# An SSM layer and a top-4 mixture of experts on one core: work moved between the last sequences and the first expert tiles

## What is computed

```python
x = layernorm(x + mamba(x))          # 16 states per feature, scan over 512 tokens
x = layernorm(x + ffn(x))

# ffn: N = 4096 tokens, E = 8 experts, INNER = 512, TOP_K = 4
logits = x @ router_weight.T + router_bias
topk_logits, topk_idx = top_k(logits, 4); topk_w = softmax(topk_logits)
gate, up = split(x @ gate_up_proj[e].T + bias)
act = (clip(up, -7, 7) + 1) * min(gate, 7) * sigmoid(1.702 * min(gate, 7))
y[token] += topk_w * (act @ down_proj[e].T + bias)   # for each chosen expert e
```

## Time and profile before

| | |
|---|---|
| three runs | 1311.96, 1314.8, 1316.92 us; median 1314.8 |
| profiled execution | 1315.4 us, its span 1313.5 us |
| busy | PE 1167.2 us (89%), DVE 1052.3 (80%), ACT 884.6 (67%), POOL 740.5 (56%) |
| mean granted TensorE clock | 0.951 of full |

### The profile page before, as it was taken

One profiled execution on the slowest core, in us unless ns is written; L12 is line 12 of the kernel. 1 busy time (PEld: TensorE's weight loads), 2 busy tenths in 40 slices (PEclk: granted clock), 3 DMA queues, 4 the chain that ended last, 5 costly groups with the idle time before them and its releaser, 6 DMA issues. The chain is left out here.

```text
span 1313.5 us, 17907 instructions
## 1 busy us (share of the span) xinstructions
PE 1167.2 (89%) x5150; PEld 805.5 (61%) x5150; DVE 1052.3 (80%) x1816; ACT 884.6 (67%) x1518; POOL 740.5 (56%) x557
## 2 busy tenths in 40 slices
PE   9879897979799897697799999999999999999960
PEld 4324353535353443256688888888888888888850
DVE  4999999999999999988477766777667776677754
ACT  4685959494949585534466776777667777667744
POOL 0456567888787888875743344443444433444353
PEclk9899998999999898897989999999999999999995
DMA  3543435445454545547665655655556555565538
GB/s 124 191 162 134 172 128 204 171 162 180 176 193 172 192 140 191 208 144 278 198 167 163 164 131 141 166 163 164 133 138 167 164 162 140 135 162 165 162 40 264
DMA packets 69260, 217.21 MB, mean 165 GB/s; under 512 B 7520, under 2 KB 43232, under 8 KB 56288
## 3 DMA queue, kind: packets, MB, share of 16 engines
q1 hardware_dynamic: 33888, 171.61, 35.8%
q0 software_dynamic: 26880, 36.72, 16.2%
q10 hardware_dynamic: 8448, 8.39, 2.0%
HBM read 165.54 MB, written 51.15 MB: 165 GB/s over the span
## 5 line engine op out<-in xcount | busy, mean ns | idle before, releaser
L662 PE MATMUL p_y<-read,small 128*128 128x512 f32 x512 | 258.1, 643 | 57.3 <-POOL read L1290 57.1
L1098 DVE TENSOR_TENSOR_SCAN state<-decay,p_bu 128x512 f32<-128x512 f32 x256 | 297.1, 1201 | 2.9 <-ACT decay L858 1.7
L1619 POOL DMA_INDIRECT total<-o_v,tok x144 | 266.8, 1853 | 43.4 <-issue 43.3
L662 PEld LDWEIGHTS p_y<-read,small 128*128 128x128 f32 x512 | 101.7, 206 | 198.5 <-issue 115.0
L1617 POOL TENSOR_TENSOR scrap<-neg_half 128x1 f32<-128x1 f32 x36 | 14.1, 392 | 313.0 <-ACT o_v L1530 310.3
L858 ACT ACTIVATE decay<-dt,scan_rate 128x511 f32<-128x511 f32 x256 | 164.1, 710 | 13.9 <-DVE state L1098 13.6
L512 ACT ACTIVATE gate_v<-p_g,bias 128x512 f32<-128x512 f32 x144 | 98.3, 683 | 99.9 <-PE p_up L502 99.5
L533 ACT ACTIVATE ah<-a_v 128x512 fp32r<-128x512 f32 x144 | 91.1, 633 | 103.4 <-DVE a_v L526 103.4
L1337 POOL DMA_INDIRECT queues<-rows,index x128 | 134.7, 1052 | 36.8 <-issue 33.6
L1290 POOL TENSOR_TENSOR read<-state,bc 128x1024 f32<-128x1024 f32 x64 | 127.5, 2001 | 23.4 <-DVE p_bu L1089 11.6
L549 DVE TENSOR_TENSOR al<-a_v,ah 128x512 fp32r<-128x512 f32 x144 | 98.5, 685 | 12.4 <-ACT ah L533 12.4
(11 more groups left out here) (234 smaller groups left out, 2992.7 us busy)
## 6 DMA issues: line engine op xcount, KB each, us to landing
bc<-bc_rows SPq DMA_DIRECT2D x32, 1024.0 KB, 4.8
first_raw<-in_w_experts SPq DMA_DIRECT2D x19, 1668.0 KB, 6.8
raw_w<-in_w_experts SPq DMA_DIRECT2D x18, 1668.0 KB, 6.8
first_wh<-bc_rows SPq DMA_DIRECT2D x16, 1024.0 KB, 4.7
first_wl<-bc_rows SPq DMA_DIRECT2D x16, 1024.0 KB, 4.7
first_rows<-queues SPq DMA_DIRECT2D x19, 544.0 KB, 6.9
xq<-queues SPq DMA_DIRECT2D x18, 544.0 KB, 6.9
queues<-pad SPq DMA_DIRECT2D x9, 544.0 KB, 5.9
```

The lines of the kernel that those rows point to most:

```text
L662: mm = pe.matmul(p_y[h][:, :], ident[:, :], read[:, t % 4, h, :], start=False, stop=(t == SLOTS - 1))
L1098: dve.tensor_tensor_scan(state[t % 4][:, h, :], decay[t % AHEAD][:, h, :], p_bu[:, h * LEN:(h + 1) * LEN], 0.0, ALU.mult, ALU.add).then_in ...
L1619: pool.indirect_dma_start(total, bass.IndirectOffsetOnAxis(ap=tok[t.p][:, a:a + 1], axis=0), o_v[t.p][:, a, :], None, compute_op=ALU.add). ...
```

## The change

- The transposed rows of tile 1 are split into halves in round LAST, slot 3: ACT's two copies ahead of the copy of product 2 of tile 0, DVE's two subtractions ahead of its clips of chunks 2 and 3. Before, both stood in chunk 1 of tile 0's part of stage 2.
- `copy_tokens` moves on DVE from chunk 0 to chunk 2 of each tile, tile 0 among them.
- POOL issues eight of the last sequence's sixteen scatters in stage 1, and the other eight (`scatter_rest`) behind the adds of tile 0.
- The spare rows of `total` have a semaphore of their own, `s_spare`; POOL's stage 2 waits for it alone and no longer for the ends.
- `write_ends` moves on SP from behind the loads of tile 2 to behind the loads of tile 3.

```diff
@@ -385,7 +385,7 @@
     LAG = 2
     s_rows = [sem(f"s_rows{i}") for i in range(2)]
     s_tr, s_tok, s_share = sem("s_tr"), sem("s_tok"), sem("s_share")
-    s_ends = sem("s_ends")
+    s_ends, s_spare = sem("s_ends"), sem("s_spare")
     s_tload, s_plan, s_tables, s_pad = sem("s_tload"), sem("s_plan"), sem("s_tables"), sem("s_pad")
     s_w = [sem(f"s_w{i}") for i in range(2)]
     s_wh, s_wl, s_bias = sem("s_wh"), sem("s_wl"), sem("s_bias")
@@ -574,7 +574,7 @@
     def write_spare_rows(sp):
 
         sp.dma_start(queues[E * QUEUE:, :].rearrange("(p a) c -> p a c", a=SUBS), pad[:, :, :]).then_inc(s_pad, 16)
-        sp.dma_start(total[TOKENS:, :].rearrange("(p a) d -> p a d", a=SUBS), pad[:, :, 0:D]).then_inc(s_pad, 16)
+        sp.dma_start(total[TOKENS:, :].rearrange("(p a) d -> p a d", a=SUBS), pad[:, :, 0:D]).then_inc(s_spare, 16)
 
     def write_ends(sp, some):
 
@@ -924,6 +924,8 @@
                     for i in (2, 3):
                         read_gate(act, first, i)
                         read_up(act, first, i)
+                    for k in range(KD):
+                        copy_tile(act, second, k)
                     copy_product(act, first, 2)
                 if r.d and t == 3:
                     router_exp(r)
@@ -1246,6 +1248,8 @@
                     rest_of_weights(dve, second, 1)
                     rest_of_product(dve, early, 0)
                     rest_of_product(dve, early, 1)
+                    for k in range(KD):
+                        rest_of_tile(dve, second, k)
                     for i in (2, 3):
                         clip_up(dve, early, i)
                         product_of_chunk(dve, early, i)
@@ -1406,7 +1410,12 @@
                 if r.c and r.b and t == 12:
                     power(r.s.at(-1), 1)
             if r.last:
-                scatter(r.s.at(-2), range(TT * TOPK))
+                scatter(r.s.at(-2), range(TT * TOPK // 2))
+
+        def scatter_rest():
+            scatter(ROUNDS[-1].s.at(-2), range(TT * TOPK // 2, TT * TOPK))
+
+        return scatter_rest
 
 
     def sp_stage1(sp):
@@ -1543,11 +1552,10 @@
                     copy_share(t, expert)
                 if i == 0 and later:
                     copy_weights(act, t.at(1), 0)
-                if i == 1:
+                if i == 1 and later:
                     for k in range(KD):
                         copy_tile(act, t.at(1), k)
-                    if later:
-                        copy_weights(act, t.at(1), 1)
+                    copy_weights(act, t.at(1), 1)
                 if i == 2 and later:
                     weigh_output(t.at(-1))
                 if i == 3:
@@ -1583,15 +1591,15 @@
                 if isinstance(t.half, int):
                     for _ in range(4):
                         next(plan, None)
-                if i == 0:
-                    copy_tokens(t)
-                    if later:
-                        rest_of_weights(dve, t, 2)
+                if i == 0 and later:
+                    rest_of_weights(dve, t, 2)
                 if i == 1 and later:
                     read_output(t.at(-1))
-                if i == 1:
+                if i == 1 and later:
                     for k in range(KD):
                         rest_of_tile(dve, t.at(1), k)
+                if i == 2:
+                    copy_tokens(t)
                 if i == 2 and later:
                     rest_of_weights(dve, t.at(1), 0)
                     rest_of_weights(dve, t.at(1), 1)
@@ -1603,7 +1611,7 @@
         read_output(Seq(ends[0], 1))
 
 
-    def pool_stage2(pool):
+    def pool_stage2(pool, scatter_rest):
         ends = []
 
         def add_output(t):
@@ -1620,12 +1628,14 @@
                                         o_v[t.p][:, a, :], None, compute_op=ALU.add).then_inc(s_add[t.p], 16)
 
         pool.wait_ge(s_scrap, SEQS)
-        pool.wait_ge(s_pad, 16 * (E + 2))
+        pool.wait_ge(s_spare, 16)
         for i in range(2):
             pool.wait_ge(s_total[i], 16 * (SEQS // 2))
         for t in tiles(pool, ends):
             if has_earlier(t):
                 add_output(t.at(-1))
+            if isinstance(t.half, int) and t.n == 1:
+                scatter_rest()
         add_output(Seq(ends[0], 1))
 
 
@@ -1654,10 +1664,10 @@
             if isinstance(t.half, int) and t.n == EARLY - 1:
                 sp.wait_ge(s_tables, 2)
                 scattered(SEQS)
-                sp.wait_ge(s_pad, 16 * (E + 2))
+                sp.wait_ge(s_pad, 16 * (E + 1))
             if has_earlier(t):
                 load(t.at(1))
-            if isinstance(t.half, int) and t.n == 1:
+            if isinstance(t.half, int) and t.n == 2:
                 sp.wait_ge(s_ends, 3)
                 write_ends(sp, range(E))
         return ends[0]
@@ -1681,8 +1691,7 @@
 
         @block.gpsimd
         def _(pool):
-            pool_stage1(pool)
-            pool_stage2(pool)
+            pool_stage2(pool, pool_stage1(pool))
 
         @block.sync
         def _(sp):
```

## The result

The changed kernel takes **1299.85 us** (median; 1298.79 to 1301.46), the kernel before 1314.41 on the same chip: ratio 0.9897, 95% interval 0.9881 to 0.9913, so 1.0% faster. Forecast was 1311.4 in a range of 1302 to 1319. The profiled execution took 1299.24 us, its span 1297.4; before it was 1315.4 and 1313.5.

The account below looks back on a forecast made before the run. PE was taken to bound the expert loop, with the room in the hand-over into it. From the profiled 1315.4 us, plus 2.5 for the hand-over and minus 6.5 for the loop gave 1311.4 us, range 1302 to 1319.

Parts of the forecast that it names:

- Step 1: Before the loop: splitting tile 1's rows earlier ends PE's 3.3 us wait; its gate/up matmuls start at 610.3 us.
- Step 2: Tile 0's token copy in chunk 2 ends at 616.1, tile 2's rows land at 620.8; PE idles from 613.1.
- the half clock: After a long PE idle in the hand-over, matmuls run at half clock; cost taken as 2.4 us.
- Step 3: Hand-over: tile 0's adds start at 636.1 instead of 645.58, amid the last scatters; the 8.2 us stall goes.
- Step 4: Hand-over: ends written behind tile 3's rows; 0.5 us lost on those rows, adds and scatters slowed by 3.0 us.
- what is late next: Tile 4's weights and rows wait for all scatters: PE idles 8.5 us, hand-over ends 2.5 us later than before.
- Step 5: Expert loop: token copy in chunk 2 makes the next weights' split earlier, closing PE's gaps: -6.5 us over 32 tiles.
- A: Hand-over: the scatters do not hold tile 4 back, its transposes start when wanted: 1300.5 us; chance 0.19.
- B: Hand-over: the 5.6 us hole in POOL's DMAs comes again, 8.2 in place of 3.0: 1316.6 us; chance 0.13.
- C: Expert loop: rows come too late for their transposes in every tile: 1366 us, or still 1337; chance 0.10.
- D: Hand-over: tile 0's adds stay late, so the 8.2 us stall remains: 1309 to 1320 us; chance 0.03.

Follow-up runs that it names:

- e1: The changed kernel with the copy of token numbers back in chunk 0 of every tile; 1311.31 us, ratio 0.9966.
- e2: The kernel before with the copy of token numbers moved to chunk 2 and nothing else of the change; 1293.86 us, ratio 0.9844.
- e3: The kernel before with the token copy still in chunk 0, but behind the split of the tile's last weights; 1301.90 us, ratio 0.9901.
- e4: The changed kernel with an unused 0.91 us memset on DVE in chunk 2 of the loop's tiles; 1323.38 us, ratio 1.0058.
- e12: The changed kernel with the loop's copies of token numbers in chunk 3 instead of chunk 2; 1462.13 us, ratio 1.1089.
- e9: The changed kernel run again with nothing altered; 1301.35 us, ratio 0.9901 to the kernel before.
- e5: The changed kernel with the token copies of tiles 0 and 1 back in chunk 0; 1300.17 us, ratio 0.9890.
- e7: The changed kernel with all sixteen scatters ahead of tile 0's adds and the ends back behind tile 2's loads; 1295.35 us, ratio 0.9848.

## Why the prediction was wrong

Times aligned to T 1 (1.7 us added to those of after) are set beside the forecast.

- **Step 1** held: the wait for xl is gone, up 1,0 starts at 610.0 (forecast 610.3).
- **Step 2** held: tok 0 at 615.9 (forecast: done by 616.1), rows 2 issued at 616.2 (616.3), PE idle 7.21 (7 to 8). The landing, bounded by 4.0 and 5.8 and taken at 4.5, was 3.9, just under the lower bound, and the half clock cost about 1.5, not 2.4 (T 2 and down 0,2 took 3.84 us, and 2.31 at full clock in the loop). The Trainium skill ("DMA: Bandwidth & Descriptors", "Anatomy of one DMA") gave 3.3 for it, an estimate by a fit that the page made for DMAs issued by GpSimd, where SP issues this one. The trace has 3.9 for this load, 0.6 above the estimate, and a median of 3.6 over all loads of rows, within 0.3 of it.
- **Step 3** held in its order: adds 0 at 635.0 (636.1), the o_v stall gone. Adds and scatters took 8.85 + 11.1 against 7.5 + 10.15 at quiet times, so 2.3 us more, where 3.0 was taken for the ends beside them. That the ends cause it is argued, not shown.
- **Step 4 and what is late next** held: rows 3 landed in 5.9 (5.8), PE idled 9.0 us before T 4 (8.5), T 4 aligned at 666.8 (667.6). In the last figure two errors meet: rows 4 left 1.6 us sooner than forecast (658.7, 660.3) and took 0.8 longer to land (8.1, 7.3). The half clock cost 2.0 there, not 2.4. The hand-over came out 1.0 us longer, the forecast 2.5.
- **Step 5 failed**, by far the largest error. The sentence that failed is "PE's idle in 500 us is 6.4, the most that there is to have". It is not the most. The profile models the ends of matmuls, these overlap the next start by 0.16 us, and so every pause is shown short by that and a pause under 0.16 not at all; nor does it count the slower first matmul. The term was -6.5 and measured **-14.9** (31 tiles x 0.48). (Even by the row cited it was short: 6.4 in 500 us makes 7.5 over 32 tiles of 18.2.) e1 (the copy back: 18.18), e2 and e3 (17.74) and e4 (0.61 per tile lost by starts, 0.35 shown) confirm it. The mechanism was the one forecast: the copy, waiting for adds, delays the split of the next weights; e3 shows that it is this work behind the copy, and e4 that a late split is enough.
- **The sum.** With -14.9 in step 5 the forecast would have been 1315.4 + 2.5 - 14.9 = 1303.0, just inside the range. The profiled execution took 3.8 less: 1.7 before T 1, which is chance between executions, 1.5 in the hand-over and 0.5 behind the loop. So step 5 made two thirds of the miss, and the rest took the result over the edge.

**The rivals.** A gave 1300.5, close to the result, for a reason that did not occur: T 4 did not start when wanted. B: adds and scatters took 2.3 us more, and the hole in POOL's DMAs came too (4.19 us), but at 615.45 to 620.62, 13 us before the ends were written. The ends are not its cause. C did not occur: in the loop rows t+2 leave at 1016.41 and are in by about 1020.0, for a transpose at 1021.94, 1.9 us of cover; e12 shows what is behind it. (Its 1366 and 1337 leave out the -6.5 that the other sums have.) D did not occur.

What the prediction missed beside the number: it found the hand-over no better and still did not ask whether the copy alone would be better than the whole. Its own chain said so: four adds of 7.5 us were put in front of the eight scatters that weights 4 wait for.

## What to carry to other kernels

Price a loop by the distance from start to start of one instruction that every iteration has; busy and idle shares from modelled ends hide part of every short pause, here half or more. Ask of a small operation on an in-order engine what stands behind it when it waits: a copy of 0.17 us cost 15 us because the split of the next weights came behind it and DVE had no slack in between. When work is pulled ahead to end a visible stall, follow what it is put in front of; here moving the waiter later did all, and moving the work that it waited for earlier gave 6 us back.

## What was not expected of the hardware

- POOL's indirect DMAs pause once near the hand-over, in all fourteen traces at the same place of the program, between the first and the second scatter of the last sequence: 5.88 us idle in the kernel before, 4.19 in the change and 2.79 in the same kernel again (e9), 1.39 in e5, 5.00 in e7, with the ends beside them or not. The cause is open.
- Pauses of 3 us in the tiles of e12 kept the granted clock at a mean of 0.89 over 500 us and cost about as much again as the pauses.
- A pause that the profile puts down to "issue" (3.16 us in e7) can be a wait for another engine: the matmul started 0.10 us behind the split that it needs, closer than the 0.13 and 0.14 of waits that the profile names.
